# A decoder of six sublayers: four edits at the head of the first two stages, and a new order of the grouped cross-attention

## The reference

```python
x = _layernorm(x + _L0_attn_ref(x, ...))         # 16 heads of 128, 4 groups, cosine-only rotation
x = _layernorm(x + _L0_xattn_ref(x, ctx, ...))   # RMS norm and rotary, causal own keys and context keys
x = _layernorm(x + _L0_ffn_ref(x, ...))          # gated MLP, 256 -> 1024 -> 256
x = _layernorm(x + _L1_attn_ref(x, ...))         # 32 heads of 8, quantised projections
x = _layernorm(x + _L1_xattn_ref(x, ctx, ctx, ...))
x = _layernorm(x + _L1_ffn_ref(x, ...))          # 8-bit product
```

```python
qh = (q @ Wq.T).reshape(N, S_, HEADS, HEAD_DIM).transpose(0, 2, 1, 3)
kh = jnp.repeat((k @ Wk.T)...., GROUP_HEADS, axis=1)
vh = jnp.repeat((v @ Wv.T)...., GROUP_HEADS, axis=1)
score = jnp.einsum('bhqd,bhkd->bhqk', qh, kh) / math.sqrt(HEAD_DIM)
attn = jax.nn.softmax(score, axis=-1)
out = jnp.einsum('bhqk,bhkd->bhqd', attn, vh)
return out.transpose(0, 2, 1, 3).reshape(N, S_, EMBED) @ Wfc.T + bfc
```

## Time and profile before

| | |
|---|---|
| runs, median (lowest to highest) | 2881.09 us (2878.8 to 2891.5) |
| the profiled execution, own time | 2885.1 us |
| its span, first to last instruction | 2883.3 us |
| mean granted clock of TensorE | 0.963 |
| busy: TensorE, VectorE, ScalarE, GpSimd | 2678.9, 1886.7, 1316.7, 1242.0 us |

### The profile page before, as it was taken

The page is one execution under the profiler, slowest core; times in us unless marked ns, Lnnn a source line. Parts: engine busy times, 40 slices in busy tenths (PEclk is TensorE's granted clock), DMA queues, the critical chain, the costliest instruction groups (busy, mean ns, idle before and its releaser), DMA issues. The chain is left out here.

```text
span 2883.3 us, 65085 instructions
## 1 busy us (share of the span) xinstructions
PE 2678.9 (93%) x23764; PEld 2312.3 (80%) x23764; DVE 1886.7 (65%) x4020; ACT 1316.7 (46%) x3143; POOL 1242.0 (43%) x1604
## 2 busy tenths in 40 slices
PE   7999999995999999999999789996999998699995
PEld 6999999984888888888888678884777776477774
DVE  6655555555777777777777554444777777366666
ACT  2222222223666666666666533332334333266655
POOL 1111121123676767676767501113545554234334
PEclk9999999998999999999999999997999999799998
DMA  5000000001000000000000010001000000000001
GB/s 180 8 7 7 4 7 7 7 8 55 6 4 5 4 5 4 5 4 5 4 5 4 18 58 0 0 0 33 9 11 7 8 11 0 26 31 25 26 12 59
DMA packets 43309, 49.18 MB, mean 17 GB/s; under 512 B 4064, under 2 KB 33632, under 8 KB 42976
## 3 DMA queue, kind: packets, MB, share of 16 engines
q1 hardware_dynamic: 43232, 48.16, 5.1%
HBM read 35.56 MB, written 4.19 MB: 14 GB/s over the span
## 5 line engine op out<-in xcount | busy, mean ns | idle before, releaser
L587 POOL TENSOR_TENSOR a_probs<-a_probs,a_rs 128x512 f32<-128x512 f32 x64 | 70.6, 1103 | 480.6 <-DVE a_rs L444 480.6
L1179 POOL TENSOR_TENSOR b_rows<-b_rows,b_swapped 128x512 f32<-128x512 f32 x160 | 204.6, 1287 | 56.9 <-DVE b_swapped L955 56.9
L1117 ACT ACTIVATE b_probs<-bank,b_shift,b_q_scale 128x128 f32<-128x128 f32 x512 | 228.4, 461 | 0.7
L1226 POOL TENSOR_TENSOR b_probs<-b_probs,b_rs 128x512 f32<-128x512 f32 x128 | 133.2, 1040 | 136.6 <-DVE b_rs L1007 133.4
L2663 ACT ACTIVATE d_probs<-d_probs 128x512 f32<-128x512 f32 x128 | 78.9, 630 | 241.0 <-DVE d_probs L2562 239.1
L532 ACT COPY a_pT<-bank 128x512 f32<-128x512 f32 x64 | 37.5, 586 | 325.8 <-PE bank L324 325.8
L1189 POOL TENSOR_TENSOR b_rms<-b_rms,sh_minus_half 128x8 f32<-128x8 f32 (+1 forms) x128 | 170.4, 1331 | 10.7
L963 DVE TENSOR_REDUCE b_ss<-b_squares 128x4 f32<-128x512 f32 x192 | 125.3, 680 | 72.8 <-ACT b_squares L1092 72.8
L46 PE MATMUL bank<-a_xT,early_wq 128*128 128x256 f32 x512 | 150.5, 294 | 12.3 <-DVE early_wq L73 10.2
L46 PE MATMUL bank<-early_wo,b_oT 128*128 128x256 f32 x512 | 149.4, 292 | 1.4 <-DVE b_oT L929 1.4
L449 DVE TENSOR_TENSOR a_oT<-bank,a_oT 128x512 fp32r<-128x512 f32 x128 | 82.6, 687 | 103.3 <-ACT a_oT L537 103.2
(11 more groups left out here) (350 smaller groups left out, 8944.6 us busy)
## 6 DMA issues: line engine op xcount, KB each, us to landing
a_xT_in<-in_xT SPq DMA_DIRECT2D x16, 256.0 KB, 2.6
sh_x<-in_x SPq DMA_DIRECT2D x1, 4096.0 KB, 18.9
b_ctx_in<-in_ctxT SPq DMA_DIRECT2D x32, 128.0 KB, 2.0
d_x_in<-sh_x SPq DMA_DIRECT2D x16, 256.0 KB, 2.3
e_x_in<-sh_x SPq DMA_DIRECT2D x16, 256.0 KB, 2.4
e_cT<-in_ctxT SPq DMA_DIRECT2D x32, 128.0 KB, 2.5
out<-sh_x SPq DMA_DIRECT2D x16, 256.0 KB, 2.1
a_qT<-in_L_attn_Wq SPq DMA_DIRECT2D x4, 512.0 KB, 5.7
```

Source lines behind the costliest of these rows:

```text
L1117: op = act.activation(probs[:, g % 2, keys], bS[:, keys], ACT.Exp, bias=shift[:, g % 2, a:a + 1], scale=q_scale[:, g, a // 2, a % 2:a % 2 ...
L1179: pool.tensor_tensor(rows[:, unit, :], rows[:, unit, :], swapped[:, half, :], ALU.add).then_inc(added[unit], 1)
L1226: pool.tensor_tensor(pr, pr, rs[:, g % 2, :].unsqueeze(2).to_broadcast([128, R, 128]), ALU.mult).then_inc(probs_ready[g], 1)
```

## The change

Five edits. In the first stage GpSimd's low part of Wo becomes 16 instructions of 128x256, and TensorE's first weighing waits for all 16. The V projection of a turn moves ahead of the last weighing of the turn before. The four small tables of the second stage get a tile of their own, loaded in the first stage. The second stage's remaining first-turn semaphores are raised by GpSimd at its start, and `v_taken` and `q_scale_ready` already in the first stage. In the fifth stage the order within a turn is a new one on TensorE, VectorE and ScalarE; GpSimd's is as before.

```diff
             def weigh_values(i, g):
                 if type(i) is int and i == 0:
-                    pe.wait_ge(wo_step, 1)
+                    pe.wait_ge(wo_step, H)
...
                 if now is not None:
                     k_proj(now)
+                    v_proj(now, 0)
+                    v_proj(now, 1)
                 if before is not None:
                     weigh_values(before, G - 1)
-                if now is not None:
-                    v_proj(now, 0)
-                    v_proj(now, 1)
...
-            pool.tensor_tensor(low, full, high.bitcast(F32), ALU.subtract).then_inc(wo_step, 1)
+            for h in range(H):
+                pool.tensor_tensor(low[:, h], full[:, h], high[:, h].bitcast(F32), ALU.subtract).then_inc(wo_step, 1)
...
-        norm_w = sb("norm_w", [128, 2, HD])
+        norm_w, cos, sin = sh.early.tables[:, 0:2, :], sh.early.tables[:, 2, :], sh.early.tables[:, 3, :]
...
-            for n, name in enumerate(("q_norm_w", "k_norm_w")):
-                sp.dma_start(norm_w[:, n, :], t["L0_xattn_" + name].rearrange("(a n) -> a n", a=1).to_broadcast([128, HD])).then_inc(tables_loaded, 16)
-            sp.dma_start(cos, t["cos_rows"]).then_inc(tables_loaded, 16)
-            sp.dma_start(sin, t["sin_rows"]).then_inc(tables_loaded, 16)
...
-            for s in looped:
-                sp.sem_inc(s, 1)
...
         @block.gpsimd
         def _(pool):
+            for s in looped:
+                pool.sem_inc(s, 1)
+
...
+        for n, name in enumerate(("q_norm_w", "k_norm_w")):
+            sp.dma_start(self.tables[:, n, :], t["L0_xattn_" + name].rearrange("(a n) -> a n", a=1).to_broadcast([128, 128])).then_inc(self.tables_loaded, 16)
+        for n, name in enumerate(("cos_rows", "sin_rows")):
+            sp.dma_start(self.tables[:, 2 + n, :], t[name]).then_inc(self.tables_loaded, 16)
+
...
-                 ("normed", 2), ("turned", 6), ("taken", 6))
+                 ("normed", 2), ("turned", 6), ("taken", 6), ("v_taken", 2), ("q_scale_ready", 0))
```

Of the fifth stage's three lists this is ScalarE's; TensorE's is shown by its instructions below, and VectorE's changes in the same way (it is the order of maxima, shifts and the two `take_att`):

```diff
             def turn(new, mid, old, oldest):
-                exponent(old, 3)
-                take_pT(old, 2, 0, False)
+                take_x(new)
                 exponent(old, 4)
-                take_x(new)
                 take_pT(old, 3, 1, False)
                 exponent(old, 5)
+                exponent(old, 6)
                 take_pT(old, 4, 2, False)
-                exponent(old, 6)
+                exponent(old, 7)
                 take_pT(old, 5, 3, False)
+                take_pT(old, 6, 4, False)
+                exponent(mid, 0)
                 take_k(new)
-                exponent(old, 7)
-                take_pT(old, 6, 4, False)
                 take_q(new)
-                exponent(mid, 0)
                 take_pT(old, 7, 5, False)
+                exponent(mid, 2)
+                exponent(mid, 3)
                 exponent(mid, 1)
-                exponent(mid, 2)
+                take_v(new, old)
                 take_pT(mid, 0, 6, True)
-                take_v(new, old)
                 take_pT(mid, 1, 7, True)
                 take_att(old)
+                take_pT(mid, 2, 0, False)
```

More of the change, by code:

```diff
@@ L647, in cross_attention_block @@
         swapped = sb("swapped", [128, 2, 512])
-        cos, sin = swapped[:, 0, 0:HD], swapped[:, 1, 0:HD]
         ss = sb("ss", [128, NU, R])
@@ L668, in cross_attention_block @@
         w_ready = nc.alloc_semaphore("b_w_ready")
-        tables_loaded = nc.alloc_semaphore("b_tables_loaded")
         masks_ready = nc.alloc_semaphore("b_masks_ready")
@@ L697, in cross_attention_block @@
         norm_step, norm_done = sem("norm_step"), sem("norm_done")
-        N_TABLES = 4
         flat = qT[:, :, :, :, :].rearrange("p g b r q -> p (g b r q)")
@@ L902, in lay_out_tables @@
             def lay_out_tables():
-                dve.wait_ge(tables_loaded, 16 * N_TABLES)
+                dve.wait_ge(sh.early.tables_loaded, 64)
                 for n in range(2):
@@ L1903, in turn @@
             def turn(new, mid, old, oldest):
[L1904 to L1907, removed]
                 turn_probs(old, 1, 0, False)
@@ L1911, in turn @@
                 turn_probs(old, 2, 1, False)
+                weigh(old, 1)
                 turn_x(new, oldest)
-                weigh(old, 1)
                 turn_probs(old, 3, 2, False)
+                weigh(old, 2)
                 project_out(oldest, mid)
                 turn_probs(old, 4, 3, False)
-                weigh(old, 2)
                 weigh(old, 3)
-                scores(mid, 0, 6, True)
+                scores(mid, 0, 7, True)
                 turn_probs(old, 5, 4, False)
+                project_k(new)
                 weigh(old, 4)
                 turn_probs(old, 6, 5, False)
-                project_k(new)
                 weigh(old, 5)
@@ L1927, in turn @@
                 weigh(old, 6)
+                project_v(new)
+                turn_probs(mid, 0, 7, True)
+                weigh(old, 7)
+                scores(mid, 1, 1, False)
             pe.wait_ge(w_loaded, 16 * sh.grouped.N_LOADS)
@@ L1983, in turn @@
             def turn(new, mid, old, oldest):
+                shift(mid, 1)
                 moments(oldest)
                 take_att(old, 1, 7)
-                maximum(mid, 7)
                 maximum(mid, 5)
@@ L1989, in turn @@
                 shift(mid, 4)
+                maximum(mid, 6)
                 shift(mid, 5)
-                maximum(mid, 6)
+                shift(mid, 6)
+                maximum(mid, 7)
                 shift(mid, 7)
-                shift(mid, 6)
+                take_att(mid, 0, 3)
                 residual(old)
-                take_att(mid, 0, 3)
+                maximum(new, 0)
                 maximum(new, 3)
+                shift(new, 0)
                 maximum(new, 2)
-                maximum(new, 0)
+                shift(new, 2)
                 maximum(new, 1)
-                shift(new, 0)
                 shift(new, 3)
-                shift(new, 2)
-                shift(new, 1)
             four_deep(dve, n_turns, turn)
@@ L2904, in __init__ @@
         self.wk, self.wv = sb("wk", [128, 2, C, 512]), sb("wv", [128, 2, C, 512])
+        self.tables = ctx.enter_context(nc.sbuf_tensor("early_tables", [128, 4, 128], F32))
+        self.tables_loaded = nc.alloc_semaphore("early_tables_loaded")
         self.loaded, self.context_loaded = nc.alloc_semaphore("early_loaded"), nc.alloc_semaphore("early_context_loaded")
```

## The result

The changed kernel took 2905.79 us (median of 7 runs, 2900.4 to 2914.29), the kernel before beside it 2883.64 (7 runs, 2878.8 to 2891.5). The ratio is 1.0074, with a 95% interval of 1.0057 to 1.0091: slower, by about 22 us, and outside the predicted range of 2863 to 2891. The profiled execution has a span of 2904.7 us against 2883.3.

A forecast was written before the change was run, and what follows sets the result against it. TensorE was taken to bound the first and grouped stages. Terms -10.1 - 2.1 + 7.4 + 1.2 = -3.6 gave 2881.5 us for a profiled execution, 2877.5 for the median, range 2863 to 2891.

The forecast's parts named there:

- What bounds the kernel: First and grouped stages: TensorE bounds both, so an edit pays only where TensorE stands still or runs at half clock.
- Edit 1: Head of first stage: Wo's low part in 16 GpSimd pieces lets VectorE in, V projection starts near 29.8; -10.1 us.
- The rival that GpSimd keeps VectorE out: Head of first stage: GpSimd holds VectorE off through all 16 pieces; total +7.5, 2888.6 us, chance 0.07.
- Edit 2: First stage: V projection ahead of the last weighing delays ScalarE about 1.5 us, covered by 2.0 us; cost 0.
- Edits 3 and 4: Second stage's start: tables loaded earlier, semaphores raised by GpSimd or earlier, first context projection starts near 686.3; -2.1 us.
- Edit 5 without the clock: Grouped stage's new order: a 1.5 us stop before transpose 1, other waits gone; +0.53 per turn, +7.4, bounds +6 to +9.
- The clock: Grouped stage: one half-clock spell in 14 turns, from one like case behind a 1.67 us stop; +1.2 us, 1.7 at most.
- The clock rival: Grouped stage: clock falls turn after turn, 1.7 us in each of 14; total +19, 2900 us, decides from 12 spells, chance 0.10.
- The tail: Grouped stage's end: 13.6 us at half clock, some 6 us lost, the same loss after the change, give or take 5.

The follow-up runs named there:

- experiments 4 to 8: Changed kernel with scores group or V projection repeated (4, 5, 7, 8); kernel before with v copies ahead of unit 0's pT (6): ratios 0.9985, 1.0117, 1.0103, 0.9981, 1.0000.
- scores_twice: Changed kernel with the second scores group computed twice, filling part of the stop: 2878.17 us, ratio 0.9985 to the kernel before.
- v_twice: Changed kernel with the V projection computed twice, ahead of the stop: 2914.20 us, ratio 1.0117 to the kernel before.
- scores_and_half: Changed kernel with half of the second scores group computed once more: 2876.19 us, ratio 0.9981 to the kernel before.

## Why the prediction was wrong

- **What bounds the kernel:** right. TensorE bounds the grouped stage, down to 221.37 busy of 221.37 us once no wait is left.
- **Edit 1, -10.1:** right in mechanism and place. Measured 9.0 at the first weighing, 11.5 at the stage's end, and 7.5 in the total (3.7 to 11.2). The pieces took 12.55 us in all, most of them 0.73, where I had 0.615 and two losses, 11.7. The rival that GpSimd keeps VectorE out is refuted: the split took 1.76. The Trainium skill, SBUF — State Buffer, section "Who interferes with whom", has the loser of the shared ports blocked for one instruction; the 1.76 agrees.
- **Edit 2, 0:** not told from it (at most 1 us). **Edits 3 and 4, -2.1:** measured -2.3.
- **Edit 5 without the clock, +7.4:** the mechanism was right, link by link (v behind weighing 7, pT of unit 0 behind v, a stop before unit 1's transpose, no wait before units 2 and 6). The size was short: +0.81 per turn, not +0.53, 11.3 for 14 turns, above my upper bound of 9. The stop is 1.57, not 1.5, and the work of a turn rose from 238.13/13 = 18.3 us to 18.49, which I had bounded at 0.12. That the waits are worth 1.1 us a turn at most was too much: without any wait the turn takes 18.45, 0.79 less than 19.24.
- **The clock, +1.2: this is the step that failed.** "I take one such spell in the 14 turns, +1.2 (1.7 at most, part of it in waits)." There were five, and they lasted 3.4 to 17.1 us and cost 1.5 to 8.0 each, nearly all of the 30.2. I went wrong twice. How often: from one like case, the half clock behind a stop of 1.67 us, I made one spell in fourteen turns. The profile of before has five stops of 1.49 to 1.99 us that began at full clock, and half clock came at the end of three of them or within 1.5 us behind it (those ending at 659.87, 667.51 and 2501.35; not 652.05 and 1640.32). How long: I took 3.41 us as what a spell lasts, while the earlier trace rows, 13.60 us at 0.50 with TensorE busy throughout, stood in the same profile and shows a spell going on under full load.
- **What I overlooked in the profile of before:** "one like case" isn't so. In its fourth stage the clock fell turn after turn, eleven spells of 3.4 or 6.8 us in fifteen turns of about 30 us. No wait of TensorE there is over 1.31 us, the typical longest of a turn is 0.99, and two of the eleven began with none over 0.41 in the 7 us before. The 13.6 us of the earlier trace rows began behind waits of 0.19, 0.19 and 0.52 within 3.5 us. TensorE in order of time and by stretch, first the fourth stage, then the grouped one's tail:

```profile
2026.73 1.05 PE L2405 MATMUL bank<-d_v,d_pT 128*64 128x18 f32 x16 [0.99 <-DVE d_att L2574]
2026.70:2030.00 3.30, 3.27 (x24) 0.50 0.00 0
...
2791.31 1.08 PE L1859 MATMUL bank<-sh_ident,e_probs 128*128 128x128 f32 x4 [0.52 <-ACT e_pT L2056]
```

  So no length of a single stop is safe everywhere: what 1.13 us did not do in the grouped stage's steady turns, 0.99 did in the fourth stage, and experiments 4 to 8 speak for the one place that they changed.
- **The clock rival** (0.10, 2900) named the mechanism and came within 6 us of the median, but by luck, by two errors that cancel: every turn at 1.7 instead of five at 5.9 on average. Its point of decision, 12 spells, was wrong for the same reason: at 8.0 each, three are enough for its 19.2 us. What I held against it, that steady turns with stops of 0.62 and 0.12 kept 1.00, was no evidence on stops of 1.5: scores_twice with 0.70 keeps it as well, and the fourth stage, with turns that lost it, was left out. The Trainium skill, TensorE: Matmul & The Clock Gate, section "A second HAM failure mode: psum-queue depth-cycling", has short idles between groups make the clock swing; v_twice and the changed kernel agree, at 1.55 us, and so does the fourth stage at 0.99, scores_and_half at 1.13 doesn't.
- **The tail, 0:** measured -4.8, of which at least part is the clock there, which differs between executions of the same turns by 5.5 us (55.2 against 49.7).

Sum by measured terms: -15.1 for all that lies ahead of the grouped stage, +0.6 + 10.5 + 30.2 - 4.8 in it, in all +21.4, the difference of the spans.

## What to carry to other kernels

Before an order is accepted that puts one longer stop of TensorE in the place of short waits, ask of that stop what the clock did after every stop near its length in the same profile, those without a fall too, count the turns that lost the clock in the other stages, and price the spell by the longest one seen, not by the shortest: here 0.8 us a turn of waiting cost 30 us of clock on top. A copy that has to wait for a late event (here v, for the weighing of two turns before) belongs behind the copy that TensorE asks for next: one line moved turned +22 us into -24 to -31. If such a stop can't be removed, work of no use in it can pay: half of one scores group computed twice won back all the clock loss inside the steady turns at no price in the turn.

## What the runs showed of the hardware that I had not expected

- The granted clock stayed at 0.50 for 17.00 us in which TensorE was busy throughout (matmul groups of 0.6 to 2 us at full clock, closely packed), after one stop of 1.56 us; after others of the same length it didn't fall, or for 3.3 us only.
- In the grouped stage the stop decided, not the work around it: 0.87 us more work in the stop of 1.57 ended the falls, 0.88 just ahead of it didn't.
- Sixteen GpSimd subtractions of 128x256 took 12.55 us where one of 128x4096 took 8.86, and let VectorE in after the first: 1.76 us for a split that had taken 9.87.
